# Splitting the normalisation before layer 3's attention into two batch halves, the first of them inside layer 2's feed-forward

## The reference, cut to what matters

```python
x = L0_attn_x
for l in range(4):
    xn = layernorm(x)
    s = attn_l(xn)                 # causal (layer 1: not causal) attention, projections in and out
    g = silu(ffn_l(xn))            # the feed-forward reads the same xn
    x = x + s * g
```

## Time and profile before

| | |
|---|---|
| Median of 3 runs | 1375.63 us (1374.1 to 1376.28) |
| The profiled execution's own time | 1388.66 us |
| Its span, first to last instruction | 1386.9 us |
| TensorE busy in the span | 1242.7 us (90%) |
| VectorE, ScalarE, GpSimd busy | 732.5, 613.1, 123.7 us |
| Mean granted TensorE clock, as a share of full | 0.961 |

### The profile page before, as it was taken

One profiled execution on the slowest core, in us unless ns is written; L12 is line 12 of the kernel. 1 busy time (PEld: TensorE's weight loads), 2 busy tenths in 40 slices (PEclk: granted clock), 3 DMA queues, 4 the chain that ended last, 5 costly groups with the idle time before them and its releaser, 6 DMA issues.

```text
span 1386.9 us, 18855 instructions
## 1 busy us (share of the span) xinstructions
PE 1242.7 (90%) x6390; PEld 777.9 (56%) x6396; DVE 732.5 (53%) x2019; ACT 613.1 (44%) x1518; POOL 123.7 (9%) x144
## 2 busy tenths in 40 slices
PE   4988888768999878999999899899999999999994
PEld 3644444442257554656565587666666666667853
DVE  4867615574134268888888640344443444446357
ACT  1734443367852214555555502344444544442053
POOL 3140012263100400000000000000000000000000
PEclk9979999869899989999999999999999999999998
DMA  8000100401112600000000001110000000000000
GB/s 214 26 16 30 44 27 0 137 33 46 46 46 73 228 0 16 13 12 12 12 9 11 1 1 72 38 39 24 20 16 23 12 24 12 24 12 1 1 0 30
DMA packets 27661, 48.64 MB, mean 35 GB/s; under 512 B 3998, under 2 KB 22398, under 8 KB 26246
## 3 DMA queue, kind: packets, MB, share of 16 engines
q1 hardware_dynamic: 25318, 38.13, 8.6%
q0 software_dynamic: 2256, 9.37, 2.3%
HBM read 40.36 MB, written 9.19 MB: 36 GB/s over the span
## 4 chain that ended last, share of the span: by engine, by line
PE 67%; DVE 13%; issue 11%; ACT 5%; POOL 3%; DMA 1%; SPq 0%; ACTq 0%; POOLq 0%; DVEq 0%
PE bank L887 12%; PE bank L903 8%; PE bank L894 8%; PE bank L880 5%; PE bank L872 5%; PE bank L898 4%; PE bank L776 3%; PE bank L760 3%; PE bank L1107 2%; PE bank L1069 2%; ACT PT L1346 2%; PE bank L1202 2%; PE bank L1125 1%; PE bank L1188 1%; PE bank L731 1%
## 5 line engine op out<-in xcount | busy, mean ns | idle before, releaser
L1232 ACT COPY R<-bank 128x512 f32<-128x512 f32 (+4 forms) x203 | 110.5, 560 | 324.3 <-PE bank L903 142.8
L1867 DVE CUSTOM_DVE_ANT_0 bank<-bank,mask_row 128x128 f32<-128x128 f32 (+3 forms) x256 | 127.0, 497 | 173.4 <-PE bank L894 170.9
L887 PE MATMUL bank<-XNT,W 128*128 128x512 f32 x416 | 200.1, 605 | 6.9 <-ACT R L1232 3.8
L1371 ACT ACTIVATE R<-bank,nm 128x128 f32<-128x128 f32 (+3 forms) x256 | 136.2, 532 | 109.0 <-DVE nm L1867 108.0
L894 PE MATMUL bank<-R 128*128 128x512 f32 (+3 forms) x384 | 134.3, 434 | 0.0
L1346 ACT ACTIVATE PT<-bank 128x512 f32<-128x512 f32 (+3 forms) x256 | 110.7, 520 | 51.1 <-PE bank L765 38.3
L887 PEld LDWEIGHTS bank<-XNT,W 128*128 128x128 f32 x416 | 75.2, 191 | 100.8 <-issue 92.8
L872 PE MATMUL bank<-W,R 128*128 128x256 f32 x576 | 125.3, 380 | 3.2 <-ACT R L1232 3.2
L872 PEld LDWEIGHTS bank<-W,R 128*128 128x128 f32 x576 | 109.1, 190 | 18.7 <-ACT R L1232 2.1
L898 PE MATMUL bank<-identf,R 128*128 128x128 f32 x640 | 112.3, 275 | 7.1 <-DVE R L1884 5.5
L903 PE MATMUL bank<-PT,R 128*128 128x128 f32 (+3 forms) x384 | 112.0, 435 | 5.6 <-ACT PT L1232 4.2
(11 more groups left out here) (257 smaller groups left out, 1782.4 us busy)
## 6 DMA issues: line engine op xcount, KB each, us to landing
W<-in_wq SPq DMA_DIRECT2D x32, 128.0 KB, 2.0
W<-in_wo SPq DMA_DIRECT2D x2, 2048.0 KB, 8.9
W<-in_egu SPq DMA_DIRECT2D x1, 2816.0 KB
W<-in_wk SPq DMA_DIRECT2D x20, 128.0 KB, 2.1
W<-in_wv SPq DMA_DIRECT2D x20, 128.0 KB, 2.1
R<-xg SPq DMA_DIRECT2D x5, 512.0 KB, 4.6
yg<-R SPq DMA_DIRECT2D x5, 512.0 KB, 3.1
W<-in_wa SPq DMA_DIRECT2D x2, 1024.0 KB, 4.8
```

The lines of the kernel that those rows point to most:

```text
L887: ins = mm(bank[:, :], wqkv23[:, s, c, :], XNT[:, c, b * SEQ:(b + 1) * SEQ], start=c == 0, stop=c == DC - 1)
L1232: return nc.scalar.copy(dst, src)
L1371: return fn(Pr[c][:, 0:n], PS[c][:, 0:n], ACT.Exp, scale=-1.0, bias=nm[:, c:c + 1], accum_out=esum[:, c:c + 1])
L1867: return dve.tensor_tensor_reduce(out=s[:, 0:n], in0=s[:, 0:n], in1=mask_row[:, SEQ - n:SEQ], scale=-1.0, scalar=-MASKED, op0=ALU.add, op1 ...
```

## The change

Layer 2's and layer 3's feed-forward, one function with branches before, become two functions, `ffn2` and `ffn3`, on each of the three engines. `ffn3` does what `ffn23(3)` did, as a hardware loop. `ffn2` is written out for both batches without a loop, and its waits are on constants.

The normalisation before layer 3 is split by batch. The statistics and scaling of tiles 0 to 3 stand on VectorE behind the last `update` of batch 0. Their transposes stand on TensorE behind the sixth hidden tile of batch 1, and their copies on ScalarE behind the sixth Gelu of batch 1. The statistics of tiles 4 to 7 stand at the end of `ffn2`. Their scaling, transposes and copies stand in `attention3` ahead of batch 1's projections, behind the first four score tiles on TensorE, the four maxima on VectorE and the first three exponents on ScalarE. The pairs of layer 3 are transposed into `PS[2]` to `PS[5]`. `attention3` waits on TensorE for the bias adds of all output tiles of `ffn2`, then before each batch's projections for that batch's pairs only.

```diff
@@ SyncE
-            sp.wait_ge(ffn[2]["f"], NT + 2)
+            sp.wait_ge(ffn[2]["f"], NT)
@@ TensorE, ln_transpose
+                    bank = PS[2 + k if l == 3 else k]
@@ TensorE, attention3
-                pe.wait_ge(xnt_ready, LN_PAIRS * 4)
+                pe.wait_ge(ffn[2]["f"], NT)
                 k = 0
                 for b in range(B):
+                    if b == 1:
+                        ln_transpose(3, (2, 3))
+                    pe.wait_ge(xnt_ready, LN_PAIRS * 3 + 2 * b + 2)
                     for kind in "qkv":
@@ TensorE, ffn2 in place of ffn23(2)
+                for b in range(B):
+                    for m in range(8):
+                        k = b * 8 + m
+                        if k >= 2:
+                            pe.wait_ge(f["act"], k - 1)
+                        for s in range(3):
+                            for c in range(DC):
+                                ins = mm(PS[m % 2][:, :], wap[:, s, c, m * P:(m + 1) * P],
+                                         x16[:, c, b * SEQ:(b + 1) * SEQ], start=s == 0 and c == 0, stop=s == 2 and c == DC - 1)
+                        ins.then_inc(f["gu_ps"], 1)
+                        if b == 1 and m == 5:
+                            ln_transpose(3, (0, 1))
+                    for t in range(TPB):
+                        tile = b * TPB + t
+                        if tile >= 2:
+                            pe.wait_ge(f["f"], tile - 1)
...
@@ all three engines, the loop over layers
-                if l != 2:
-                    ln_transpose(l)
+                if l < 2:
+                    ln_transpose(l)
@@ ScalarE, attention3
                 for b in range(B):
+                    if b == 1:
+                        ln_copy(3, (2, 3))
                     for kind in "qkv":
@@ ScalarE, ffn2 in place of ffn23(2)
+                for b in range(B):
+                    for m in range(8):
+                        act.wait_ge(f["gu_ps"], b * 8 + m + 1)
+                        fn(h2[:, m, :], PS[m % 2][:, :], ACT.Gelu, bias=bias2[:, m:m + 1]).then_inc(f["act"], 1)
+                        if b == 1 and m == 5:
+                            ln_copy(3, (0, 1))
...
@@ VectorE, attention3
                 for b in range(B):
+                    if b == 1:
+                        ln_scale(3, 1)
                     store_k(b, 3 * b + 1, PS[7 - b])
@@ VectorE, ffn2 in place of ffn23(2)
+                for tile in range(NT):
+                    dve.wait_ge(f["y_ps"], tile + 1)
+                    if tile >= 2:
+                        dve.wait_ge(f["g"], tile - 1)
+                    tt(fpost16[tile % 2], PS[6 + tile % 2][:, 0:D], bout, ALU.add).then_inc(f["f"], 1)
+                    if tile % TPB:
+                        update(tile - 1)
+                    if tile % TPB == TPB - 1:
+                        b = tile // TPB
+                        update(tile)
+                        dve.wait_ge(f["xup"], TPB * (b + 1))
+                        ln_stats(3, b)
+                        if b == 0:
+                            ln_scale(3, 0)
```

More of the change, by code:

```diff
@@ L1171, in shared1, with ffn2, ffn3 @@
                     ins.then_inc(f["y_ps"], 1)
[L1173 to L1178, removed]
+            def ffn2():
+                f = ffn[2]
+                pe.wait_ge(xb_ready, 2)
+                pe.wait_ge(parts_ready, 1)
+                for b in range(B):
[15 more added lines that the diff above has]
+                        for m in range(8):
+                            if t == 0:
+                                pe.wait_ge(f["act"], b * 8 + m + 1)
+                            for s in range(3):
+                                ins = mm(PS[6 + t % 2][:, 0:D], h2[:, m, t * P:(t + 1) * P], wbp[:, s, m, :],
+                                         start=m == 0 and s == 0, stop=m == 7 and s == 2)
+                        ins.then_inc(f["y_ps"], 1)
+            def ffn3():
+                f = ffn[3]
+                pe.wait_ge(parts_ready, 2)
                 with pe.Fori(0, B) as b:
@@ L1183, in ffn23 @@
                             for c in range(DC):
[L1184 to L1188, removed]
+                                ins = mm(PS[m % 2][:, :], ta[:, c, m * P:(m + 1) * P],
+                                         xp3[:, s, c, bass.ds(b * SEQ, SEQ)], start=s == 0 and c == 0, stop=s == 2 and c == DC - 1)
                         ins.then_inc(f["gu_ps"], 1)
@@ L1223, in _ @@
                     out_projection(l, OT23, wo23, NH)
-                    ffn23(l)
+                    (ffn2, ffn3)[l - 2]()
         @block.scalar
@@ L1538, in ffn23 @@
                         act.wait_ge(f["gu_ps"], b * 8 + m + 1)
[L1539 to L1556, removed]
+                        act.wait_ge(f["h"], b * 8 + m + 1)
+                        fn(h3p[:, 0, m, :], PS[m % 2][:, :], ACT.Gelu, bias=bias3[:, m:m + 1],
+                           scale=small[:, 48:49])
+                        fn(h3f[m % 4], PS[m % 2][:, :], ACT.Gelu, bias=bias3[:, m:m + 1],
+                           scale=small[:, 48:49]).then_inc(f["act"], 1)
+                for k in range(NT // 2):
+                    act.wait_ge(f["f"], 2 + NT + k + 1)
+                    y = y3[:, 2 * k:2 * k + 2, :]
+                    fn(y, y, ACT.Silu).then_inc(f["g"], 1)
             for l in range(4):
-                if l != 2:
+                if l < 2:
                     ln_copy(l)
@@ L2071, in shared1, with ffn2, update @@
                 ln_stats(2, 1)
[L2073 to L2094, removed]
+            def ffn2():
+                f = ffn[2]
+                dve.wait_ge(corea[0]["o_ps"], NH * B)
+                for src, p in ((wa, wap.rearrange("p s c n -> p s (c n)")),
+                               (wb, wbp.rearrange("p s m n -> p s (m n)"))):
+                    own(cp(p[:, 0], src))
+                    own(tt(wres, src, p[:, 0], ALU.subtract))
+                    own(cp(p[:, 1], wres))
+                    own(tt(p[:, 2], wres, p[:, 1], ALU.subtract))
+                dve.sem_inc(parts_ready, 1)
+                def update(tile):
+                    g = gpost[tile % 2]
+                    dve.wait_ge(f["g"], tile + 1)
+                    own(tt(g, g, S[:, tile, :], ALU.mult))
+                    tt(X[:, tile, :], X[:, tile, :], g, ALU.add).then_inc(f["xup"], 1)
+                for tile in range(NT):
+                    dve.wait_ge(f["y_ps"], tile + 1)
+                    if tile >= 2:
+                        dve.wait_ge(f["g"], tile - 1)
[9 more added lines that the diff above has]
+                            ln_scale(3, 0)
@@ new lines, in ffn3 @@
+            def ffn3():
+                f = ffn[3]
+                dve.wait_ge(corea[1]["o_ps"], NH * B + 2)
+                ternarise()
+                x = XNT[:, :, :].rearrange("p c t -> p (c t)")
+                p = xp3.rearrange("p s c t -> p s (c t)")
+                own(cp(p[:, 0], x))
+                own(tt(xres, x, p[:, 0], ALU.subtract))
+                own(cp(p[:, 1], xres))
+                own(tt(p[:, 2], xres, p[:, 1], ALU.subtract))
+                dve.sem_inc(parts_ready, 1)
+                dve.sem_inc(f["h"], 4)
@@ L2120, in ffn23 @@
+                    third(7)
                     for t in range(TPB):
                         dve.wait_ge(f["y_ps"], b * TPB + t + 1)
[L2122 to L2136, removed]
+                        tile = b * TPB + t
+                        stt(y3[:, tile, :], PS[6 + t % 2][:, 0:D], small[:, 49:50], bout, ALU.mult, ALU.add).then_inc(f["f"], 1)
+                        dve.wait_ge(f["f"], tile + 1 + 2)
+                        dve.tensor_reduce(rstd[:, bass.ds(tile, 1)], y3[:, tile, :], AX.X, ALU.max,
+                                          apply_absolute_value=True).then_inc(f["mul"], 1)
```

59 lines of the change are left out of this document (26 added, 33 removed).

## The result

The changed kernel takes 1366.7 us, the median of 5 runs (1364.98 to 1370.09), where the kernel before takes 1375.24 us (5 runs, 1374.1 to 1376.28). The ratio is 0.9939 with a 95% interval of 0.9922 to 0.9957, which is 5.9 to 10.7 us. Two later measurements, on two chips where both kernels are slower, gave 0.9929 (0.9905 to 0.9952) and 0.9943 (0.9921 to 0.9964); beside the second of them one slow run of the kernel before, at 3863 us, is left out. The forecast was 1369.8 us, 5.8 us of gain, with a range from 1368.0 to 1372.8. The direction was right and the gain too small by 2 to 3 us.

What follows compares the result with a forecast made beforehand. TensorE, busy 90% of the span, was taken as the bound, with a 6.47 us stop and half-clock transposes. Terms -0.2 + 0.9 + 0.5 + 11.25 = 12.45 us against 18.23 gave 5.8 us off 1375.63: 1369.8 us, range 1368.0 to 1372.8.

Steps and rivals of the forecast that it cites:

- the terms of the turn: From layer 2's last output tile to batch 1's q projection in layer 3: 12.45 us instead of 18.23, gain 5.8 us.
- The feed-forward's last output tile: Layer 2's feed-forward start: the loop's first wait for ScalarE's queue goes, -0.2 us, bounds 0 and -0.2.
- The eight transposes inside the feed-forward: First half's transposes in batch 1 of layer 2's feed-forward: no wait, 0.9 us, upper bound 1.9 at half clock.
- The wait for the bias add: New wait of `attention3` on TensorE between last output tile and first projection: 0.5 us, bounds 0.45 and 0.8.
- From batch 0's to batch 1's q projection: Layer 3's start: batch 0's projections, score tiles, then the second half's scaling, transposes and copies, 11.25 us together.
- The stop behind the score tiles: TensorE stands still about 1.85 us before the second half's transposes, behind batch 0's fourth score tile.
- The rest: Layer 3's heads and `ffn3` keep their instructions and order: 0 us.
- rival A: TensorE's clock falls at the new stop behind the score tiles: 1.4 us more, 1371.2 us; chance 0.25.
- Rivals B and C: TensorE instructions late during `wa3`/`wb3` load, up to 6.9 us, chance 0.07; written-out code fed too slowly, 15.8 us lost, 0.04.
- Rival D: First half not ready in time, or VectorE's statistics push the maxima: each 1 us, to 1370.8; chance 0.08.
- The profile's 13 us over the median: Profiled execution is 13.0 us above the plain runs' median; assumed not in this stretch, so 5.8 came off 1375.63.

## Why the prediction was too small

**What bounds it, the terms of the turn: right, within 0.3 us.** The feed-forward's last output tile, without the new transposes, came 0.3 us earlier, for 0.2 forecast and 0.2 as the bound. The eight transposes inside the feed-forward took 0.87 us for 0.9 forecast, without a wait. The wait for the bias add was 0.52 for 0.5. From batch 0's to batch 1's q projection it was 11.07 us for 11.25. The stop behind the score tiles was ended by VectorE's scaling, as said, and was 1.44 us long where about 1.85 were forecast, mostly because the score tiles ended 7.6 us and not 7.4 behind the first projection and the scaling started 0.2 us sooner. Batch 1's q projection came 6.1 us earlier, of which 5.8 had been worked out.

**"*The rest.* Layer 3's heads and `ffn3` keep their instructions and order: 0" failed.** They kept both, and still took 1.7 us less than in the profile that the prediction rested on. I had read the clock's windows only where TensorE stood still and where it came back, and priced the fall there by the 16 transposes. The fall in layer 3's feed-forward stood in the same trace, in the 10.03 us of 75 matmuls between 1336 and 1347, and I hadn't asked whether a shift ahead of it would undo it. Over five profiles before pays this 1.7 us each time, at the turn or there; the changed kernel paid it once in six. So the term was not 0 but 1.7 us of gain. With it the sum is 6.1 + 1.7 = 7.8 us, and off the 1375.24 measured for before the time is 1367.4, against 1366.7 measured. The 0.7 us left are within the scatter.

**The range was too narrow for this reason.** It had a price for the clock falling once more, in rival A, and none for a fall that goes. The other end should have had the same 1.7 us. Its arithmetic doesn't come out either: the terms named give 1369.7 at the lower end, not 1369.3, and 1.1 us more to each side makes 1368.6 to 1372.3.

**Rival A** came in one of six profiles of the changed kernel, at its place and nearly at its price: 1.8 us (582.8 for 581.0) where 1.4 were written. Three more profiles have the same new stop, those with two and six matmuls added and the one with the first half behind the last tile, and with them it came in two of nine. The chance of 0.25 was fair. In this case's profiles a fall is the exception for stops of 1.44 and 0.67 us. Behind the stop of 6.3 or 6.5 us the 16 transposes took 3.7 us, half the full clock, in all seven profiles that have it.

**Rivals B and C**, late instructions during the loads, didn't happen: between 886 and 892 the DMA engines moved 363 GB/s and TensorE was busy all the time. The kernel that was only written out had a ratio of 0.9995, no slower than before.

```profile
886.00:890.00 4.00, 4.00 (x21) 2.56 (x20) 2.91 (x11) 0.60 (x1) 1.27 (x2) 1.00 0.90 363
...
890.00:892.00 2.00, 2.00 (x12) 1.43 (x11) 1.09 (x5) 1.53 (x2) 0.00 (x0) 1.00 0.91 364
```

**Rival D** didn't come: `XN` was ready at 867.61 + 1.38 = 869.0, 1.3 us ahead of the transposes, for 1.2 forecast. The statistics didn't push the maxima either: the last was read 8.44 us behind the first projection, as before.

**The profile's 13 us over the median** were taken for a cost of that execution. They seem to go with the chip, by the two groups of profiles above, and so to lie ahead of the change. Taking the gain off the median was right all the same.

Open is why the kernel before pays its 1.7 us, in five profiles of five, at one of two places that lie 430 us apart. That the arrival at the stops decides whether the clock falls is what the added matmuls speak for, with one profile on each side. What ties the two places together no run shows.

## What to carry to other kernels

Compare two profiles from a common instant just ahead of the change to the end, and not by their spans: here 12.3 of 20 us came from elsewhere. Go through the clock's windows of the whole trace before calling untouched code free of charge, since short stops behind the change can lose or gain a fall of the clock, here probably because they came at another time. When a normalisation is split by halves, put the second half's steps on every engine ahead of the work that can wait: the order on VectorE and ScalarE was worth 2.0 us in the profile, though the medians could not tell it.

## What the runs showed of the hardware

Two stops of 1.04 and 0.56 us, the same in every kernel here, bring TensorE's clock down in some executions and not in others: in three of five profiles of the kernel before, in none of six of the changed one. With 0.43 us more work ahead of them it stayed at 2.4 GHz in a profile of the kernel before, and with 2.60 us more it fell to 1.2 GHz in one of the changed kernel, which speaks for the time at which they come. The price was 1.67 us in all four profiles in which it fell there.

The same code takes longer up to layer 2's output projection on some chips than on others (791 to 802 against 782 to 787 us, about 11 us on average), while the stretch behind it agrees: the five profiles of the changed kernel without a fall, from chips of both groups, have 580.9 to 581.0 us.
